# The second layer norm's tiles split into float16 halves as token rows and transposed by DMA

## What is computed

```python
def ffn(x):                                   # weights rounded to float8_e4m3fn
    gate = silu((x @ q(gate_w)) * gate_scale)
    up   = (x @ q(up_w)) * up_scale
    return ((gate * up) @ q(down_w)) * down_scale

# x: (4, 512, 512) float32; token_ids pick one of four experts e for a token
h   = layernorm(x)
x   = x + tanh(g_xattn) * where_expert(e, (silu(h @ M[e].T) * (h @ M[e].T)) @ M[e].T)
x   = x + tanh(g_ffn)   * ffn(layernorm(x))   # 512 -> 1536 -> 512
```

## Time and profile before

| | us |
|---|---|
| median of 3 runs | 435.64 |
| lowest, highest | 433.06, 437.16 |
| span of the profiled execution, first to last instruction | 435.9 |
| TensorE busy in it | 393.6 |
| VectorE, ScalarE, GpSimd busy | 232.9, 190.3, 172.3 |

### The profile page before, as it was taken

The page is one execution under the profiler, slowest core; times in us unless marked ns, Lnnn a source line. Parts: engine busy times, 40 slices in busy tenths (PEclk is TensorE's granted clock), DMA queues, the critical chain, the costliest instruction groups (busy, mean ns, idle before and its releaser), DMA issues. The chain is left out here.

```text
span 435.9 us, 6949 instructions
## 1 busy us (share of the span) xinstructions
PE 393.6 (90%) x1991; PEld 199.1 (46%) x2013; DVE 232.9 (53%) x479; ACT 190.3 (44%) x306; POOL 172.3 (40%) x209
## 2 busy tenths in 40 slices
PE   3358999999999999799989999999999999999991
PEld 3235545555555555344434444444444444444440
DVE  6567888777776678677642422232432224323234
ACT  3567566757776765766342222222222222222220
POOL 3335479644585537799630430000710001700003
PEclk9999999999999999999989999999999999999997
DMA  4762410110121021133000010000100000200002
GB/s 175 260 241 75 144 50 25 51 48 24 48 71 54 25 96 48 52 96 89 10 0 0 26 72 2 0 0 2 72 24 0 0 0 0 96 2 1 2 0 96
DMA packets 10507, 22.64 MB, mean 52 GB/s; under 512 B 1624, under 2 KB 1648, under 8 KB 10480
## 3 DMA queue, kind: packets, MB, share of 16 engines
q1 hardware_dynamic: 7920, 13.92, 10.2%
q0 software_dynamic: 2560, 8.39, 5.6%
HBM read 18.11 MB, written 4.19 MB: 51 GB/s over the span
## 5 line engine op out<-in xcount | busy, mean ns | idle before, releaser
L1321 PE MATMUL bank<-X,W 128*128 128x512 f16 (+1 forms) x768 | 174.6, 381 | 0.3 <-DVE late_norms L1084 0.3
L1321 PEld LDWEIGHTS bank<-X,W 128*128 128x128 bf16 x768 | 75.3, 98 | 91.9 <-issue 1.9
L1093 DVE SCALAR_TENSOR_TENSOR cs<-bank,up_mul,cs 128x512 f32<-128x512 f32 x48 | 36.0, 749 | 112.2 <-PE bank L1321 105.3
L1328 PE MATMUL bank<-W,cs 128*128 128x512 bf16 x355 | 86.9, 381 | 3.2 <-DVE cs L1101 2.1
L682 ACT ACTIVATE cs<-bank,gate_mul 128x512 f32<-128x512 f32 x48 | 32.9, 685 | 81.1 <-PE bank L1321 78.7
L527 POOL TENSOR_TENSOR xs<-xs,X 128x512 f32<-128x512 f32 x12 | 15.3, 1273 | 125.6 <-DVE X L1140 125.3
L689 ACT ACTIVATE cs<-cs 128x512 f16<-128x512 f32 x47 | 29.5, 628 | 74.8 <-DVE cs L1093 74.8
L1328 PEld LDWEIGHTS bank<-W,cs 128*128 128x128 f16 x376 | 36.5, 98 | 46.2 <-DVE cs L1101 2.6
L1101 DVE TENSOR_TENSOR cs<-cs 128x512 f16<-128x512 f32 x47 | 33.9, 721 | 36.7 <-ACT cs L689 35.9
L483 POOL TENSOR_TENSOR w_sum<-ws,w_big 128x512 f32<-128x512 f32 x36 | 47.1, 1309 | 4.7 <-DVE w_big L892 2.5
L486 POOL TENSOR_TENSOR W<-w_sum,w_big 128x512 bf16<-128x512 f32 (+1 forms) x36 | 46.9, 1303 | 3.4 <-POOL w_sum L483 1.1
(11 more groups left out here) (149 smaller groups left out, 433.4 us busy)
## 6 DMA issues: line engine op xcount, KB each, us to landing
cs<-in_ctx SPq DMA_DIRECT2D x4, 1024.0 KB, 7.9
ws<-in_L_ffn_gate_w SPq DMA_DIRECT2D x12, 256.0 KB, 2.6
ws<-in_L_ffn_up_w SPq DMA_DIRECT2D x12, 256.0 KB, 2.6
ws<-in_L_ffn_down_w SPq DMA_DIRECT2D x12, 256.0 KB, 2.7
dsc<-in_L_ffn_down_scale SPq DMA_DIRECT2D x1, 256.0 KB
xs<-in_x,order POOLq DMA_INDIRECT x16, 6.9
out<-xs,order POOLq DMA_INDIRECT x16, 2.7
ids<-in_itok_BxS SPq DMA_DIRECT2D x1, 8.0 KB, 1.6
```

What stands on the lines that cost most here:

```text
L1093: v.scalar_tensor_tensor(out=fuse[:, c % 2, :], in0=UP[c % 2][:], scalar=up_mul[:, c:c + 1], in1=sg[:, c % 2, :], op0=ALU.mult, op1=ALU.mu ...
L1321: ins = t_.matmul(dst[c % 2][:], w, x2_group(g, part, k), start=(k == 0 and part == 0), stop=(k == KC - 1 and part == 1))
L1328: ins = t_.matmul(ACC[t][:], fuse_part(g, c, part)[:, t * P:(t + 1) * P], W8[:, down_slab(c), :], start=(c == 0 and part == 0), stop=(c == ...
```

## The change

ScalarE and VectorE now make the float16 halves from `x2n` itself, in token rows, into a new buffer `x2rows` with two slots (high half in the first 512 columns, low half in the next). SP then issues one DMA a tile, `dma_start_transpose`, from a slot's 128 x 1024 float16 into `X2`, in the layout that it had. TensorE's transposes of `x2n` are gone. The order of SP's queue is written out: in a step the slab loads that the step's sums set free, then the turn of tile s-6; after the steps the turns of tiles 13, 14 and 15, each behind one more slab load. ScalarE waits in `x2_high` for the DMA that last read its slot, TensorE before the first group for tiles 0 to 3 and before the second for all. `normalise2` waits for `x2lo_done` instead of `x2T_done`. The counts of `acc_free` start at zero.

```diff
+        x2rows = sb("x2rows", [P, 2, 2 * D], F16)
...
-        def x2_part(tile, part):
-            if isinstance(tile, int):
-                return X2[:, tile // TPG, part, :, tile % TPG, :]
...
+        def x2_row(lo, part):
+            return x2rows[:, lo % 2, part * D:(part + 1) * D]
+
+        def x2_columns(tile):
+            v = X2[:, tile // TPG, :, :, tile % TPG, :]
+            return v.rearrange("p a k i -> p (a k) i")
+
+        def x2_landed(engine, tile):
+            for slot in range(2):
+                engine.wait_ge(x2T_in[slot], 16 * ((tile - slot) // 2 + 1))
...
-            for n in range(2, SLABS):
+
+            def turn_x2(tile):
+                sp.wait_ge(x2lo_done, tile + 1)
+                sp.dma_start_transpose(x2_columns(tile), x2rows[:, tile % 2, :]).then_inc(x2T_in[tile % 2], 16)
+
+            load_slab(2)
+            load_slab(3)
+            loaded = 4
+            for s in range(STEPS):
+                for n in slabs_of(s, s):
+                    nxt = min(m for m in range(loaded, SLABS + 1) if m == SLABS or slab_before(m) is not None)
+                    if nxt < SLABS and slab_before(nxt) <= n:
+                        load_slab(nxt)
+                        loaded = nxt + 1
+                if s >= X2_LAG:
+                    turn_x2(s - X2_LAG)
+            tile = TILES - 3
+            for n in range(loaded, SLABS):
                 load_slab(n)
+                if tile < TILES:
+                    turn_x2(tile)
+                    tile += 1
...
                 if not (isinstance(tile, int) and tile == 0):
-                    act.wait_ge(x2T_done, tile)
+                    act.wait_ge(x2lo_done, tile)
...
-            def x2_high(tile, src):
-                act.wait_ge(x2T_done, tile + 1)
-                a.activation(x2_part(tile, 0), src[:].rearrange("p (k i) -> p k i", k=KC),
-                             ACT.Copy, scale=X_SCALE).then_inc(x2hi_done, 1)
+            def x2_high(tile, lo):
+                act.wait_ge(x2n_done, tile + 1)
+                if not (isinstance(tile, int) and tile < 2):
+                    act.wait_ge(x2T_in[lo % 2], (tile - lo % 2) * 8)
+                a.activation(x2_row(lo, 0), x2n[:], ACT.Copy, scale=X_SCALE).then_inc(x2hi_done, 1)
...
-            def x2_low(tile, src):
-                return x_low(x2_part(tile, 1), src[:].rearrange("p (k i) -> p k i", k=KC), x2_part(tile, 0),
-                             x2hi_done, tile + 1)
+            def x2_low(tile, lo):
+                return x_low(x2_row(lo, 1), x2n[:], x2_row(lo, 0), x2hi_done, tile + 1)
...
-            def turn_x2(tile, dst):
-                pe.wait_ge(x2n_done, tile + 1)
-                if not (isinstance(tile, int) and tile == 0):
-                    pe.wait_ge(x2lo_done, tile)
-                transpose4(dst, x2n, x2T_done)
...
-                if lo >= X2_LAG:
-                    turn_x2(s - X2_LAG, X2T)
...
-            pe.wait_ge(xlo_done, STEPS)
-            turn_x2(TILES - 3, XT)
             pe.wait_ge(norms_read, 1)
+            x2_landed(pe, TPG - 1)
             gate_up(0, 0)
             product_y(STEPS - 1, (code >> 2) & 3)
-            turn_x2(TILES - 2, XT)
             gate_up(0, 1)
-            turn_x2(TILES - 1, XT)
             gate_up(0, 2)
...
+                if first:
+                    x2_landed(pe, TILES - 1)
                 gate_up(g + 1, 0)
```

More of the change, by code:

```diff
@@ L184, in build @@
         bank = [stack.enter_context(nc.psum_tensor(f"bank{i}", [P, 512], F32)) for i in range(8)]
-        Z, HT, XT, Y, X2T, SMALL = bank[0], bank[1], bank[2], bank[3], bank[4], bank[6]
+        Z, HT, XT, Y, M0_SUM, SMALL = bank[0], bank[1], bank[2], bank[3], bank[4], bank[6]
         MT_SECOND = [bank[4], bank[3], bank[5], bank[7]]
@@ L243, in build @@
         x2n_done = sem("x2n_done")
-        x2T_done = sem("x2T_done")
+        x2T_in = [sem("x2T_in0"), sem("x2T_in1")]
         x2hi_done = sem("x2hi_done")
@@ L280, in slab_tile @@
             return v.rearrange(pat).bitcast(F32)[:, t * D:(t + 1) * D]
-        def x2_part(tile, part):
-            if isinstance(tile, int):
-                return X2[:, tile // TPG, part, :, tile % TPG, :]
-            return X2[:, ds(tile >> 2, 1), part, :, ds(tile & 3, 1), :].rearrange("p a k b i -> p (a k b) i")
+        def x2_row(lo, part):
[6 more added lines that the diff above has]
+                engine.wait_ge(x2T_in[slot], 16 * ((tile - slot) // 2 + 1))
         def x2_group(g, part, k):
@@ L525, in _ @@
                 if t < TILES - TPG:
-                    pool.wait_ge(acc_free, TPG + t + 1)
+                    pool.wait_ge(acc_free, t + 1)
                     g.tensor_tensor(xs[:, t, :], xs[:, t, :], slab_tile(t // TPG, t % TPG),
@@ L650, in step @@
                 if lo >= X2_LAG:
-                    x2_high(s - X2_LAG, X2T)
+                    x2_high(s - X2_LAG, lo)
                 for i, n in enumerate(squared_of(s, lo)):
@@ L708, in _ @@
             late_abs(0)
-            x2_high(TILES - 3, XT)
+            x2_high(TILES - 3, TILES - 3)
             gate_silu(0, 0)
@@ L713, in _ @@
             fuse_high(0, 0)
-            x2_high(TILES - 2, XT)
+            x2_high(TILES - 2, TILES - 2)
             normalise2(TILES - 1)
@@ L717, in _ @@
             gate_silu(0, 1)
-            x2_high(TILES - 1, XT)
+            x2_high(TILES - 1, TILES - 1)
             fuse_high(0, 1)
@@ L760, in expert_scale @@
                 dve.wait_ge(msum_done, e + 1)
-                src = X2T[:, 0:1] if e == 0 else SMALL[:, M_SUM + e:M_SUM + e + 1]
+                src = M0_SUM[:, 0:1] if e == 0 else SMALL[:, M_SUM + e:M_SUM + e + 1]
                 link(v.tensor_scalar(m_sum[:, c], src, 2.0 ** -40, 2.0 ** 80,
@@ L1038, in step @@
                 if lo >= X2_LAG:
-                    x2_low(s - X2_LAG, X2T).then_inc(x2lo_done, 1)
+                    x2_low(s - X2_LAG, lo).then_inc(x2lo_done, 1)
                 if lo == STEPS - 1:
@@ L1102, in unit_low @@
                                 ALU.subtract).then_inc(fl_done, 1)
-            x2_low(TILES - 3, XT).then_inc(x2lo_done, 1)
+            x2_low(TILES - 3, TILES - 3).then_inc(x2lo_done, 1)
             late_slabs(0)
@@ L1111, in _ @@
             unit_low(0, 0)
-            x2_low(TILES - 2, XT).then_inc(x2lo_done, 1)
+            x2_low(TILES - 2, TILES - 2).then_inc(x2lo_done, 1)
             unit_fuse(0, 1)
-            x2_low(TILES - 1, XT).then_inc(acc_free, TPG)
+            x2_low(TILES - 1, TILES - 1).then_inc(x2lo_done, 1)
             unit_low(0, 1)
@@ L1141, in group @@
                     if last:
-                        dve.wait_ge(acc_free, TPG + g * TPG + t + 1)
+                        dve.wait_ge(acc_free, g * TPG + t + 1)
                         v.tensor_tensor(xs[:, g * TPG + t, :], xs[:, g * TPG + t, :], slab_tile(g, t),
@@ L1194, in expert_sum @@
                     pe.wait_ge(mscale_done, e)
-                dst = X2T[:, 0:1] if e == 0 else SMALL[:, M_SUM + e:M_SUM + e + 1]
+                dst = M0_SUM[:, 0:1] if e == 0 else SMALL[:, M_SUM + e:M_SUM + e + 1]
                 t_.matmul(dst, ones32[:], part_ssq[:, e:e + 1], start=True,
@@ L1337, in down @@
                     if c == 0:
-                        pe.wait_ge(acc_free, g * TPG + t + 1)
+                        if isinstance(g, int) and g == 0:
+                            pe.wait_ge(x1_done, STEPS)
+                        else:
+                            pe.wait_ge(acc_free, (g - 1) * TPG + t + 1)
                     ins = down_tile(g, c, t)
```

## The result

The kernel after takes 442.14 us, the median of 4 runs (439.42 to 443.63), against 435.05 us for the kernel before on the same chip: ratio 1.0166, 95% interval 1.0125 to 1.0207. So the change costs 7 to 8 us. The forecast was 434.2 us, no change that can be told. The time lies inside the range; the direction is wrong.

What follows compares the result with a forecast made beforehand. TensorE, 90% busy, was taken to bound the kernel, in the steps too. Transposes gone -3.5, SBUF inputs +0.5 and late slabs +1.6 made -1.4 us: 435.6 to 434.2 us, range 428 to 458 us.

Steps and rivals of the forecast that it cites:

- Here TensorE sets the pace: Steps, 77 to 166 us: TensorE, 94% busy, bounds them, while VectorE, ScalarE and GpSimd have a quarter or more free.
- Transposes gone, -3.5 us: Steps: each tile's removed TensorE transposes are worth 0.44 us, of which 3.5 us in all arrives; nothing after the steps.
- normalise2 behind x2_low, "so nothing": Steps: ScalarE's normalise2 starts about 1.4 us later, at no cost because ScalarE is idle 27 of 89 us.
- the sum: Whole kernel: -3.5 + 0.5 + 1.6 = -1.4 us, taken from 435.6 us to give 434.2 us.
- Two SBUF inputs, +0.5 us, between 12 ns and 0.77 us each: VectorE's low-half operation reading both inputs from SBUF beside GpSimd: 0.5 us slower in all, between 0 and 2.
- The crossbar DMA, 4.0 us to landing, SP's issue 0.33 us: SP queue: each transpose lands in 4.0 us, between 2.6 and 8.1, and its issue costs no more than a load's.
- B: Rival, chance 0.22: last two slabs late behind slow transposes, slower from about 6 us landing; 444 us at 8.1.
- C: Rival, chance 0.18: crossbar or SP saturates, deciding from 6.3 us of occupancy; at 10.4 us a transpose, about 500 us.
- Slabs 26 and 27, +1.6 us: After the steps: these loads stand behind transposes; slab 27 lands 1.6 us late, costing 1.6 us, between 0 and 8.6.
- the prediction's sign: Test of the forecast near 182 us: ScalarE's wait for a slab is 1 to 2 us.
- Clock, "no change": Up to 213 us: TensorE's granted clock stays at 1.00, the 2.4 GHz level, since it remains as busy as before.
- Rival A: Chance 0.16: all of TensorE's saved time arrives, in the steps and after them, giving about 428.5 us.

Runs made afterwards that it cites:

- b_all: Kernel before with normalise2 waiting for x2_low, x2_low reading unused SBUF, and dummy crossbar transposes; TensorE's transposes kept: 440.17 us, 1.0142.
- two_x2n: Kernel after with two x2n buffers, so normalise2 may run one tile ahead: 439.96 us, 1.0078.
- psum_x2n: Kernel after with x2n written to a PSUM bank instead of SBUF, all computed: 435.22 us, 1.0044.
- b_sq: Kernel before with ScalarE's squares moved ahead of x2_high, TensorE's transposes kept: 430.28 us, 0.9914.
- sq_two: Kernel after with two x2n buffers and ScalarE's squares moved ahead of x2_high: 431.93 us, 0.9952.
- b_wait: Kernel before with one edit, normalise2 waiting for x2_low of the tile before instead of TensorE's transpose: 436.31 us, 0.9991.
- b_wait_sbuf: Kernel before with normalise2 waiting for x2_low and x2_low reading its float32 operand from unused SBUF, no DMA added: 440.3 us, 1.0138.
- b_sbuf: Kernel before with x2_low in the steps reading its float32 operand from unused SBUF instead of PSUM: 436.53 us, 1.0054.
- b_dma: Kernel before with dummy crossbar transposes of unused memory, in the kernel after's queue order: 435.08 us, 1.0008.
- late_turns: Kernel after with the crossbar transposes of tiles 14 and 15 issued behind the last two slab loads: 439.01 us, 1.016.
- after_again: Kernel after measured once more, nothing changed: 442.56 us, 1.0171.
- sq_psum: Kernel after with x2n in a PSUM bank and ScalarE's squares moved ahead of x2_high: 433.37 us, 0.9964.

## Why the prediction was wrong, point by point

*What bounds the kernel.* "Here TensorE sets the pace" was the first wrong step. Busy 94% it was, and in steps 8 and 10 it does set the pace, matmul behind matmul. But at the end of each odd step its program waits for ScalarE's squares, then turns to the next pair, and what comes next is the turn of h. From the end of the squares to that turn it takes 2.0 to 2.2 us ahead of step 8, 1.9 to 2.1 ahead of step 10, 1.5 to 1.6 ahead of 12 and 18, 1.1 to 1.2 ahead of 14 and 1.9 to 2.0 ahead of 16, in all eighteen profiles, whatever was edited (101.05 to 102.97 before, 98.41 to 100.45 after). Part of that is hidden under the matmuls still running; the rest is the idle time called issue, 1.00 and 0.77 us ahead of steps 8 and 10 before, 1.44 and 1.27 after. So an odd step ends by ScalarE's clock. What TensorE's program spends the 1.9 us on no view shows.

*Transposes gone, -3.5 us.* The size on TensorE was right, 0.44 us each; the arrival was wrong. The prediction let the even step's transpose arrive in part (0.25 us) and the odd step's in full (0.44). The steps by themselves, from one turn of h to the next, us:

```
step          8      9     10     11
before      6.63   7.53   6.62   7.16
after       6.32   8.45   6.34   8.29
b_all       6.62   8.30   6.75   8.04
two_x2n     6.32   7.85   6.31   7.36
psum_x2n    6.29   7.80   6.29   7.32
b_sq        6.62   7.05   6.62   6.68
sq_two      6.18   7.16   6.19   6.67
```

The even step's did arrive, some 0.3 us, and 0.44 with the squares early. The odd step's did not: that step ends by the squares, and with the squares at their old place it is longer by about what the even one gained. What is left is 0.07 and 0.17 us a pair in psum_x2n, 0.11 at most in two_x2n, and nothing in the times of b_all against the kernel after. The whole loss of the kernel after in these steps lies in the odd ones (+0.92 and +1.13). I had looked at the room ahead of xn in the odd step, and not at what ends the head of the even one.

*normalise2 behind x2_low, "so nothing".* This is the step that failed worst. By itself the verdict is right (b_wait, 0.9991). I argued from ScalarE's idle time, 27 of 89 us, an average, where the question was how long it may be late at that one place: before it waited 15.0 us in twelve steps for TensorE's turn of h right behind x2n, 1.25 us each. The order uses up this slack: in b_wait ScalarE waits 15.2 us for x2_low, and 7.0 in place of 23.4 us for the turn of h over the whole execution. What comes on top counts. What it cost in the change as made is the difference between b_wait_sbuf and b_sbuf: 1.0138 against 1.0054, some 3.6 us where the sum had nothing.

*Two SBUF inputs, +0.5 us, between 12 ns and 0.77 us each.* The slowdown was 0.49 us each on average, nearer to the upper bound than to the 12 ns; the median of L1101 misled, since most of its 47 run after 224 us, where GpSimd is 32 of 212 us busy, and not 51 of 89. GpSimd lost as well, 1303 to 1427 ns a difference over the whole kernel. Alone this is 0.5% (b_sbuf), nearly all of it in the tail. The two terms together are 1.4%, because x2_low's extra time lands on a ScalarE without slack. I had added two terms that cost more together than their sum.
The Trainium skill, SBUF — State Buffer, section SBUF: two separate sides, says that a VectorE operation with two SBUF inputs and a GpSimd operation that reads SBUF take one shared port pair in turn, each for its whole instruction. The runs agree: the shortest x2_low of the kernel after is 0.64 us, the longest 1.76, which is 0.68 and a wait shorter than one GpSimd operation of 1.27. It would have been a reason to take the upper bound.

*The crossbar DMA, 4.0 us to landing, SP's issue 0.33 us.* 3.3 us to landing (3.0 to 4.5), so B's and C's condition, 6 us or more, never came near. The count of pieces was right: 16896 packets more are 1056 a transpose, and 1024 were reckoned. Their price was not. From 166 to 190 us the DMA view of the kernel after has (packets, MB, share of 16 engines)

```profile
q1 hardware_dynamic: 5008, 2.49, 45.6%
```

That is 175 us of engine time; less six slabs of 128 packets at 99 ns, 99 us are left for four transposes. That makes an estimate of 23 ns a piece, and each transpose holds the sixteen engines for 1.5 us, where the upper bound had 99 ns and 6.3 us. The weakest point was weak: the issue takes 1.24 us of SyncE,

```profile
100.77 1.24 SPq L403 DMA_TRANSPOSE X<-x2rows  x1
```

four times a load's, but SyncE has that time. The Trainium skill's rule of Advanced Engine Details and Errata, X-Bar Transpose (TRN2), as fast as regular DMAs, was close: 3.3 us against 2.7 to 3.0 for slabs of as many bytes in the same kernel. By that rule the sum would have been 432.6 us, not the 432.1 that the prediction gives, since the 0.5 us of the splits stay in it. The Trainium skill's 1309 ns a block (VectorE: DVE Perf Modes, The three transpose paths) doesn't add up block by block here: eight of them would be 10.5 us.

*Slabs 26 and 27, +1.6 us.* The tail did grow by 1.7 us, but ScalarE's wait for slab 27 is only 0.82 us in the kernel after (0.37 in b_dma), under the 1 to 2 us of the prediction's sign, and the cause is another: b_dma has the same order of loads and no longer tail, late_turns has them earlier and no shorter one, b_sbuf has 1.16 us of it with no DMA. That the +1.6 of the sum matches is luck.

*Clock, "no change".* Wrong in some runs: in after_again the clock fell behind the wait of step 13, which cost 2.6 us in the pair 14 to 16 (16.76 against 14.19).

*The sum.* The span of 435.9 us, which it takes for a time like the medians, is not one: the run of the kernel after with a span of 437.7 us took 439.42. This changes nothing in the terms.

So the range held 442.14 us only because it had been drawn wide for B, a late slab by slow DMAs; that the time lies in it is luck. Rival A didn't happen, B and C priced DMAs, and what the runs showed instead, ScalarE held by VectorE, had been dismissed in one clause.

What stays open: why the kernels with a crossbar and the squares early (0.9945 to 0.9964) don't reach b_sq, with 0.4 us a pair in their favour. Their longer tails (65.1 to 66.4 us against 64.67) and the low clock behind step 13 speak for themselves, but their share in the times was not separated. With x2n in PSUM TensorE also waits 1.8 us for x2_low in the tail (psum_x2n and sq_psum), by the wait that was added there.

## What to carry to other kernels

- An engine that is busy 94% need not set the pace in every stretch. Look for its last wait before the loop turns over, and whose work that waits for. Here two instructions of ScalarE, swapped, gave 0.9%, with the transposes left where they were.
- When an edit moves a wait, measure the slack at that place (how long the waiting engine idles next, for whom), not its idle share. Test costs in pairs as well as alone: nothing and 0.5% made 1.4%.
- An operand moved from PSUM to SBUF can cost VectorE and GpSimd together more busy time (here 5.9 and 4.6 us) than TensorE is relieved of (7.0). Keeping x2n in PSUM took back three quarters of the loss (1.0171 to 1.0044).

## What the runs showed of the hardware that I had not expected

- VectorE's fp32 operation with one PSUM and one SBUF input (x2_low, 128x512) takes 0.68 us beside a busy GpSimd, with two SBUF inputs 1.17 on average and up to 1.76; a GpSimd operation beside it goes from 1.27 to 1.78.
- A crossbar transpose of 128x1024 float16 from SBUF to SBUF lands in 3.3 us and takes SyncE 1.24 us to issue. Sixteen of them raise the DMA packets from 10507 to 27403 and cost the kernel before nothing that can be measured (1.0008).
- After about 2 us of near idleness TensorE ran at the 1.2 GHz level for over 6 us in one profile of the kernel after (wait 2.06 us) and not in the other (1.88 us); in b_dma it did so for some 3 us behind a wait of 0.61 us, and in late_turns not behind one of 2.09.
